# Summing the quantised context over its rows on VectorE ahead of one matmul with ones

## What is computed

```python
    def fake_quant(x, scale, zp):
        s = scale.reshape(())
        z = zp.reshape(())
        q = jnp.clip(jnp.round(x / s + z), QMIN, QMAX)
        return (q - z) * s
    q1 = fake_quant(x1, x1_scale, x1_zp)
    q2 = fake_quant(x2, x2_scale, x2_zp)
    return jnp.matmul(q1, q2)
...
    x = x + _L0_xattn_ref(_layernorm(x, axis=-1), ctx_4096, L0_xattn_x1_scale, ...)
```

## Time and profile before

| | |
|---|---|
| median of 3 runs | 2093.88 us (2090.14, 2093.88, 2093.97) |
| the profiled execution | 2090.67 us, span 2088.9 us |
| TensorE matmul busy | 2029.1 us, 97% |
| VectorE busy | 1601.9 us, 77% |
| ScalarE busy | 1006.3 us, 48% |
| GpSimd busy | 690.7 us, 33% |
| TensorE clock, mean granted | 0.993 |

### The profile page before, as it was taken

The page is one execution under the profiler, slowest core; times in us unless marked ns, Lnnn a source line. Parts: engine busy times, 40 slices in busy tenths (PEclk is TensorE's granted clock), DMA queues, the critical chain, the costliest instruction groups (busy, mean ns, idle before and its releaser), DMA issues.

```text
span 2088.9 us, 25557 instructions
## 1 busy us (share of the span) xinstructions
PE 2029.1 (97%) x9140; PEld 1526.0 (73%) x9144; DVE 1601.9 (77%) x2880; ACT 1006.3 (48%) x1418; POOL 690.7 (33%) x481
## 2 busy tenths in 40 slices
PE   8999999999889999999999999999999999999899
PEld 6777786877757777777777766777777777776587
DVE  5886786667677888888888887788888888888544
ACT  3432331222365555565555655555556555556300
POOL 1342342501134343433433333333333343333300
PEclk9999999999999999999999999999999999999899
DMA  7443553322988787786877898878687786877612
GB/s 269 167 164 117 181 171 98 130 68 81 330 167 179 140 191 166 145 183 137 187 170 151 193 237 215 195 151 184 140 181 169 147 188 139 184 151 146 187 61 71
DMA packets 654942, 341.11 MB, mean 163 GB/s; under 512 B 574720, under 2 KB 591360, under 8 KB 652768
## 3 DMA queue, kind: packets, MB, share of 16 engines
q1 hardware_dynamic: 654816, 339.48, 67.7%
HBM read 152.76 MB, written 44.04 MB: 94 GB/s over the span
## 4 chain that ended last, share of the span: by engine, by line
PE 82%; DVE 7%; DMA 5%; ACT 2%; issue 2%; POOL 2%; SPq 1%; DVEq 0%; ACTq 0%
PE ps L43 27%; PE ps L45 26%; PE ps L44 26%; PE ps L809 1%; DMA raw<-in_ctx 1%; POOL u_sb L1936 1%; DMA pT<-pp 1%; DVE t_sb L1151 1%; DVE pp L1504 1%; DVE psb L1487 1%; DMA raw<-in_W 1%; DVE vhl_sb L1222 0%; DVE u_sb L1151 0%; DMA raw<-in_ctxT 0%; PE ps L816 0%
## 5 line engine op out<-in xcount | busy, mean ns | idle before, releaser
L1504 DVE SCALAR_TENSOR_TENSOR pp<-psb,st,pp 128x1024 f16<-128x1024 f32 x256 | 411.2, 1606 | 4.8 <-ACT pp L1832 2.8
L1825 ACT ACTIVATE psb<-psb,st 128x1024 f32<-128x1024 f32 x256 | 295.0, 1152 | 238.3 <-DVE st L1490 238.2
L1487 DVE CUSTOM_DVE_ANT_0 psb<-ps,mask 128x1024 f32<-128x1024 f32 x256 | 313.4, 1224 | 115.9 <-PE ps L45 108.6
L1832 ACT ACTIVATE pp<-psb,st 128x1024 f16<-128x1024 f32 x256 | 294.0, 1149 | 142.5 <-DVE st L1499 137.6
L1960 POOL TENSOR_TENSOR wol<-araw,woh 128x512 fp32r<-128x512 f32 x128 | 166.7, 1303 | 447.6 <-ACT woh L1784 447.6
L1960 POOL TENSOR_TENSOR wql<-araw,wqh 128x512 fp32r<-128x512 f32 x128 | 165.0, 1289 | 346.5 <-ACT wqh L1784 346.5
L1151 DVE TENSOR_TENSOR x_lo<-ps,x_lo 128x512 f32<-128x512 f32 x264 | 181.0, 686 | 47.5 <-PE ps L45 47.3
L43 PE MATMUL ps<-woh,osb 128*128 128x512 f32 x512 | 201.4, 393 | 7.4 <-DVE x_lo L1151 4.0
L43 PE MATMUL ps<-ksb,qsb 128*128 128x512 f32 x512 | 200.4, 391 | 7.9 <-DVE st L1487 4.8
L43 PE MATMUL ps<-pT,vsb 128*128 128x512 f16 x512 | 195.2, 381 | 9.9 <-DMA pT<-pp 9.7
L44 PE MATMUL ps<-wol,osb 128*128 128x512 f32 x512 | 199.8, 390 | 0.0
(11 more groups left out here) (252 smaller groups left out, 4069.5 us busy)
## 6 DMA issues: line engine op xcount, KB each, us to landing
araw<-in_wq SPq DMA_DIRECT2D x128, 256.0 KB, 4.7
araw<-in_wo SPq DMA_DIRECT2D x128, 256.0 KB, 4.4
k_scratch<-khl SPq DMA_DIRECT2D x32, 512.0 KB, 3.6
ksb<-k_scratch SPq DMA_DIRECT2D x16, 1024.0 KB, 6.1
raw<-in_wv SPq DMA_DIRECT2D x16, 512.0 KB, 4.7
raw<-in_ctxT SPq DMA_DIRECT2D x16, 512.0 KB, 4.6
raw<-in_wk SPq DMA_DIRECT2D x16, 512.0 KB, 5.5
raw<-in_ctx SPq DMA_DIRECT2D x16, 512.0 KB, 4.8
```

Of the source, the lines that this page charges most:

```text
L1487: e.tensor_tensor_reduce(out=psb[:, n % 3, :], in0=pair(n % 2 * 2), in1=mask[:, i, :], scale=1.0, scalar=LOWEST, op0=ALU.add, op1=ALU.max, ...
L1504: e.scalar_tensor_tensor(out=pp[:, r, 1024:2048], in0=psb[:, r, :], scalar=st[:, n // 4 % 4, 16 + i:17 + i], in1=pp[:, r, 0:1024], op0=ALU ...
L1825: e.activation(P, P, ACT.Exp, bias=c[:, 4 + i:5 + i], accum_out=c[:, 8 + i:9 + i]).then_inc(a_exp.sem, 1)
L1832: e.activation(pp[:, r, 0:1024], psb[:, r, :], ACT.Copy, scale=st[:, n // 4 % 4, 16 + i:17 + i]).then_inc(a_ph.sem, 1)
```

## The change

The matrix of ones becomes half precision. VectorE adds each quantised tile, from the second tile of a batch on, to a running sum of 128x1024 in half precision, which lies in the upper half of `ctab`'s 4 KB per partition, seen as 16-bit values. The first addition adds tiles 0 and 1, the other six add a tile to the sum. Each waits for the tile and for the sum before it, both written by VectorE itself; the first one of batch 1 also waits for the last read of batch 0's `ctab`. TensorE runs one matmul of ones per half on the sum instead of eight on the tiles, and waits for the last addition. Half precision holds integers up to 2048 in size exactly, so the sums are the same.

```diff
--- before.py
+++ after.py
@@ -164,7 +164,7 @@
     ts_sb = alloc(one, "ts_sb", [128, 2, 512], F32R)
     l0 = ExitStack()
     identb = alloc(l0, "identb", [128, 128], BF16)
-    onesb = alloc(l0, "onesb", [128, 128], BF16)
+    onesb = alloc(l0, "onesb", [128, 128], F16)
     bq = alloc(l0, "bq", [128, 8, 1024], BF16)
     a1T = alloc(l0, "a1T", [128, 8, 512], BF16)
     a_sb = alloc(l0, "a_sb", [128, 2, 1024], BF16)
@@ -263,6 +263,10 @@
             return spare[:, hl, :]
         return slots[:, s if s < 6 else s - 1, hl, :]
 
+    def sums():
+
+        return ctab[:, 512:1024].bitcast(F16)
+
     def vhl(o, hl):
         return vhl_sb[:, o, hl, :]
 
@@ -392,6 +396,7 @@
     v_q = signal("v_q", quantised)
     v_a = signal("v_a", range(8))
     v_rows = signal("v_rows", range(2))
+    v_cs = signal("v_cs", [n for n in range(16) if n % 8])
     v_bq = signal("v_bq", [f"x{n}" for n in range(16)])
     v_ctab = signal("v_ctab", [(b, nh) for b in range(2) for nh in range(2)])
     v_l0 = signal("v_l0", [(b, n, j) for b in range(2) for n in range(8) for j in range(2)])
@@ -791,14 +796,14 @@
         def l0_product(b):
             e.wait_ge(a_a1T.sem, a_a1T[4 * b + 3])
             e.wait_ge(v_bq.sem, v_bq[f"x{8 * b + 7}"])
+            e.wait_ge(v_cs.sem, v_cs[8 * b + 7])
             if b == 0:
                 e.wait_ge(d_const["onesb"].sem, 16)
             else:
                 e.wait_ge(v_l0.sem, v_l0[0, 7, 0])
             for nh in range(2):
-                for k in range(8):
-                    m = e.matmul(bank(4 + nh), onesb[:, :], bq[:, k, nh * 512:nh * 512 + 512], start=k == 0, stop=k == 7)
-                m.then_inc(t_l0.sem, 1)
+                e.matmul(bank(4 + nh), onesb[:, :], sums()[:, nh * 512:nh * 512 + 512], start=True, stop=True).then_inc(
+                    t_l0.sem, 1)
             for n in range(8):
                 i, nh = n // 2, n % 2
                 if n in (1, 2):
@@ -1244,6 +1249,14 @@
                 e.wait_ge(t_l0.sem, t_l0[0, 7])
             e.wait_ge(v_q.sem, v_q["x", n])
             e.tensor_scalar(bq[:, n % 8, :], q, MAGIC + 255.0, -(MAGIC + 128.0), ALU.min, ALU.add).then_inc(v_bq.sem, 1)
+            if n % 8:
+                if n == 9:
+
+                    e.wait_ge(v_l0.sem, v_l0[0, 7, 0])
+                if n % 8 > 1:
+                    e.wait_ge(v_cs.sem, v_cs[n - 1])
+                e.wait_ge(v_bq.sem, v_bq[f"x{n}"])
+                tt(sums(), bq[:, 0, :] if n % 8 == 1 else sums(), bq[:, n % 8, :], ALU.add).then_inc(v_cs.sem, 1)
 
         def l0_end(b):
             rows = R[:, 4 * b:4 * b + 4]
@@ -2043,7 +2056,7 @@
     arrays = {
         "identf": np.eye(128, dtype=np.float32),
         "identb": np.eye(128).astype(ml_dtypes.bfloat16),
-        "onesb": np.ones((128, 128), ml_dtypes.bfloat16),
+        "onesb": np.ones((128, 128), np.float16),
         "x": f["x"].reshape(8, 128, 1024),
         "ctx": ctx.reshape(2, 8, 128, 1024),
         "ctxT": ctx.transpose(0, 2, 1).reshape(2, 8, 128, 1024),
```

## The result

The median went from 2092.53 us to 2100.44 us, a ratio of 1.0034 with a 95% interval of 1.0024 to 1.0044: 7.1 us slower, 5.0 to 9.2 (the ratio times the median of before, as everywhere below; the medians differ by 7.9). The forecast was 4.45 us slower, 2098.3 us on the median, with 5 in 10 for no change. By the bound that the prediction set for "no change", 0.2%, the kernel became slower, which it had put at 0.43. One of the 14 executions took 9277.59 us, and one of the kernel with the change in batch 0 alone 2938.29; both are left out of the ratios. Two more measurements of the same kernel, beside other runs of before, gave 1.0036 (1.0022 to 1.0050) and 1.0036 (1.0023 to 1.0048). The profiled execution took 2097.16 us, 6.5 more than that of before; its span is 2095.4 us.

The account below looks back on a forecast made before the run. Batch 0 was taken as bound by a chain of VectorE, GpSimd, ScalarE and loads, with TensorE only just keeping pace. Terms: 4.4 + 1.7 - 1.65 = +4.45 us, giving 2098.3 us on the median, range 2091 to 2105.

Parts of the forecast that it names:

- What bounds the stage: Batch 0: a chain of VectorE, GpSimd, ScalarE and loads decides; TensorE, 97% busy, only just keeps pace.
- The additions on the path: Batch 0: four additions in the chain, 0.72 us each, plus 1.5 us of GpSimd delays make ctab 4.4 us later.
- GpSimd's turns: Batch 0: additions of tiles 2, 4, 6 each make GpSimd's khl about 0.5 us late, 1.5 us in three turns.
- The clock: Behind batch 0's wait for ctab, grown from 2.54 to 5.7 us, the lowered granted clock costs 1.7 us more.
- Batch 1: Second batch's product: VectorE 1.6 us late at ctab, TensorE's second group 1.65 us earlier, so 1.65 us gained.
- The sum: Whole kernel: 4.4 + 1.7 - 1.65 = +4.45 us, 2098.3 us on the median.
- the second rival: VectorE's additions run at the fp32 rate or GpSimd gets its turn first: +7 to +11 us; chance 0.2.
- the faster one: Path goes over TensorE, VectorE has slack in both batches: -6.05 us at most, or -1.65 to -3.0; chance 0.1.
- The additions are dear: VectorE's additions run at the fp32 rate or GpSimd goes first: 2101 to 2105 us; chance 0.2.
- The first rival: Batch 0: the clock is not lost, or clashes with GpSimd don't come: +1.5 to +2.7 us; chance 0.25.

Follow-up runs that it names:

- the additions alone: Changed kernel with all 16 matmuls of ones per batch back on the tiles, the additions' sum unused; against the kernel before 1.0023, again 1.0022.
- the matmuls alone: Kernel before with only the first of eight matmuls of ones per half and no additions; 0.9992 against before, -1.7 us.
- table early with batch 1: Kernel before with batch 0's ctab written ahead of the split of w13, plus the change in batch 1; 0.9987 against before.
- batch 1 only: The change in batch 1 alone, batch 0 summing with eight matmuls per half as before; 0.9988 against before, -2.5 us.
- the additions late: Changed kernel with batch 0's seven additions moved into one row behind the rotation of s = 22; 1.0006 against before, +1.3 us.

## Why the prediction was right or wrong

**What bounds the stage** was right. The chain through VectorE, GpSimd, ScalarE and the loads sets the time of batch 0, and TensorE's 97% misleads: 28 matmuls less gave -1.7 us alone. Each of the waits named in advance is there: 1.20, 0.87 and 1.35 us ahead of s = 14, 18 and 22 (1.3 was said).

**The additions on the path**: 4.4 us was said for the load of w13 and for ctab, and it was right within 1 us. The store ahead of that load was 3.5 to 4.4 later than 139.80 in the three profiles of the changed kernel, and 4.2 and 4.7 in those of the additions alone. At the second group 2.4 to 3.3 and 3.2 to 4.4 seem to be left against 153.94. But in that profile of before the small operation ahead of ctab took 1.33 us, and 0.23 in all three of the changed kernel. Against the other profile of before (152.94, with 0.23) the changed kernel is 3.4 to 4.3 later, and the additions alone are 4.2 and 4.4 later than the profile of before with the same duration. For the same reason the wait for ctab was 4.41 to 4.58 us and not 5.7; with 1.33 there, in batch 0 alone, it was 5.33. An addition holds VectorE 0.80 instead of 0.72 us: between its start and the end of the write before it lie not 0.03 but 0.10 us. It waits for two things there; the first addition, which waits for the tile alone, starts 0.04 behind (57.71).

**GpSimd's turns** were right in kind and size: khl takes 0.46 longer (1.76 for 1.30), 0.5 was said, and in the changed kernel GpSimd never came first: every addition takes 0.69. With the additions in one row it did once, and that addition took 1.66.

**The clock**: 1.7 us were counted once, for batch 0, and that was about right there. In the three profiles the product of batch 0 lost 2.9, 1.6 and 1.4 us behind waits of 4.41, 4.50 and 4.58, and over its executions the kernel with batch 0 alone loses 1.7 us more than before. The whole change loses some 3; that the rest is batch 1's is seen in one of its three profiles. That a wait of 2.5 us is free was read from one place, and it doesn't hold each time: behind 2.24, 2.38 and 2.42 us the clock fell, behind 2.20, 2.36 and the 2.54 of before it did not.

**Batch 1** is the term that was mis-sized: 1.65 us gained was said; 0.9, 1.0 and -3.1 came in the changed kernel. VectorE began the table 14.85 us after the transposes behind s = 50 (the row below), where it could have begun 12.47 after them before (329.09 and 316.62); 2.4 us later and not 1.6. Of the difference 0.5 is the 0.08 of six additions, and the small operation L1264 ahead of the table took 0.72 where it was 0.22. TensorE stood waiting 1.9 to 3.0 us where the sum has 1.4. The prediction priced that wait by its length alone and not by the clock, though it had just done so for batch 0. That is the step that failed: behind the 3.04 us of one profile the product took 14.82 us instead of 11.91, which is more than the whole gain.

```profile
336.59 0.72 DVE L1264 TENSOR_SCALAR small<-small,scal 128x4 f32<-128x4 f32 x1
337.23 1.51 DVE L1267 TENSOR_SCALAR ctab<-ps,scal 128x512 f32<-128x512 f32 x2
```

**The sum**: 4.45 us against 7.1 to 7.5. Batch 0 was put at 4.4 + 1.7 = 6.1 and came at 5.2 by the time of batch 0 alone; s = 24 was 3.9 to 5.4 later than in the first profile of before, 4.9 to 6.4 later than in the second. So that half was if anything put too high. From s = 24 to s = 53 the changed kernel took 0.5 and 0.6 less and 3.5 more than before, 0.8 more on average, where 1.65 less was said; that is 2.4 us missed. By the marks of s = 53 the three profiles are 6.0 us later on average than the two of before. The remaining 1 to 1.5 us are not located: behind s = 53 single profiles scatter by more. The measured 7.1 to 7.5 lies outside the forecast's own +3 to +6, at the lower edge of what the second rival gives (+7 to +11), though not by that rival's cause. And the forecast gave "no change" more chance than "slower", because it sat on the bound.

**The rivals**: the faster one (TensorE bounds) is refuted by the matmuls alone. "The additions are dear" is refuted in its cause, they take 0.69. The first rival, that the clock isn't lost or the clashes don't come, is refuted by the granted clock of 0.50 and by khl's 1.76; and the additions alone, whose executions lose no more to the clock than those of before, cost 4.6 to 4.8 us.

The Trainium skill ("VectorE: DVE Perf Modes", The perf-mode tier table) gave the 16-bit addition an estimated 0.69 us; the trace agrees with 0.69, for two bfloat16 inputs as for half precision with bfloat16. The Trainium skill ("GPSIMD Engine Reference", 1. Specifications) names contention with a VectorE instruction of two SBUF inputs; the trace agrees, with 1.76 us for 1.30.

## What to carry to other kernels

Work moved off the busiest engine is no gain where that engine keeps pace with a loop of the others only just: follow the chain back from the wait next to the change, and put the moved work where the receiving engine stands idle, not into the loop. Here the place was worth 6 us, and the same additions in the idle place, with the matmuls taken away, came to +1.3 us, which can't be told from nothing. Price a new wait of TensorE twice, by its length and by the clock behind it. And look first at what the waiting engine waits for: an order on the other engine may give more than the work taken away.

## What the hardware showed

The granted clock falls behind waits of TensorE that are shorter than the prediction took for harmless, and not each time. From the second group on, the product takes 11.91 us at full clock. Behind waits of 3.04 and of 4.33 to 5.33 us it took 13.3 to 14.9, in six cases of six, over both batches and all profiles; behind 1.50 to 1.93 us it took 11.91 in five of five. In between, from 2.20 to 2.54 us, it is open: three times 13.5 to 13.6 (2.24, 2.38, 2.42), three times 11.91 (2.20, 2.36, 2.54). Three of these in batch 1, of the table early with batch 1, batch 1 only and the additions late:

```profile
329.61 12.26 PE L823 MATMUL ps<-bq,a1T 128*128 128x512 bf16 x55 [2.20 <-DVE ctab L1276]
...
332.05 12.26 PE L823 MATMUL ps<-bq,a1T 128*128 128x512 bf16 x56 [2.36 <-DVE ctab L1276]
...
334.23 13.86 PE L814 MATMUL ps<-bq,a1T 128*128 128x512 bf16 x55 [2.38 <-DVE ctab L1269]
```

An addition on VectorE with two inputs from SBUF made a GpSimd operation of 1.30 us that started 0.07 behind it last 1.76. A small VectorE operation of 0.23 us took 1.33 in some profiles, with a GpSimd operation of 1.26 us that started 0.04 to 0.05 behind it, and 0.23 in others with the same distance. Seven additions in a row took 6.96 us, from 142.75 to 149.71; the last six 1.04 each on average, where 0.80 was the price of one elsewhere. GpSimd ran two operations in that time (1.79 and 1.67 us).
